# Splitting a constants load, swapping eight start-up products for six, and dropping one tiny product from a convolution loop

## What is computed

```python
x = x + attn(cond(x, cond_1024, Wx, Wh, b), A_log, D, C_re, C_im, log_dt)
x = x + ffn(cond2(x, cond_1024, W_f, b_f, W_i, b_i, W_h, b_h), router_w, ..., sw_down)
```

## Time and profile before

| what | us |
|---|---|
| median of 3 executions | 961.59 |
| lowest, highest | 960.31, 963.49 |
| profiled execution, whole | 963.19 |
| its span, first to last instruction | 961.4 |

### The profile page before, as it was taken

One profiled execution on the slowest core, in us unless ns is written; L12 is line 12 of the kernel. 1 busy time (PEld: TensorE's weight loads), 2 busy tenths in 40 slices (PEclk: granted clock), 3 DMA queues, 4 the chain that ended last, 5 costly groups with the idle time before them and its releaser, 6 DMA issues.

```text
span 961.4 us, 62897 instructions
## 1 busy us (share of the span) xinstructions
PE 914.8 (95%) x27872; PEld 760.5 (79%) x27873; DVE 405.3 (42%) x781; ACT 506.7 (53%) x1735; POOL 300.6 (31%) x324
## 2 busy tenths in 40 slices
PE   7999999999999999999999999999899999999993
PEld 5887888888888888995444446788799999999993
DVE  1000000000000004552999799775555646556450
ACT  2444444444444446543876776235456656566551
POOL 3111111111111112540004473760055464554545
PEclk7799999999999999999999999999999999999997
DMA  2222223221111111111001120532466576665634
GB/s 90 83 94 93 97 90 116 88 75 40 36 33 33 41 39 37 66 66 47 0 1 45 44 71 11 208 125 78 154 141 136 132 163 128 150 136 131 134 39 54
DMA packets 69161, 80.34 MB, mean 84 GB/s; under 512 B 24225, under 2 KB 53558, under 8 KB 69122
## 3 DMA queue, kind: packets, MB, share of 16 engines
q1 hardware_dynamic: 54242, 62.18, 20.4%
q0 software_dynamic: 14592, 17.10, 10.8%
q10 hardware_dynamic: 288, 0.56, 0.2%
HBM read 44.16 MB, written 33.83 MB: 81 GB/s over the span
## 4 chain that ended last, share of the span: by engine, by line
PE 88%; DVE 4%; ACT 3%; issue 2%; POOL 1%; DMA 0%; POOLq 0%; SPq 0%; ACTq 0%; DVEq 0%
PE ps L517 22%; PE ps L817 17%; PE ps L831 9%; PE ps L509 9%; PE ps L683 8%; PE ps L733 6%; PE ps L489 4%; PE ps L760 3%; PE ps L583 2%; PE ps L596 2%; PE ps L605 2%; PE ps L742 2%; PE ps L494 2%; ACT tok L885 1%; PE ps L569 1%
## 5 line engine op out<-in xcount | busy, mean ns | idle before, releaser
L517 PE MATMUL ps<-tok,wh 128*32 128x8 f32 x16384 | 262.2, 181 | 12.4 <-ACT tok L885 5.7
L517 PEld LDWEIGHTS ps<-tok,wh 128*32 128x32 f32 x16384 | 216.5, 112 | 65.0 <-ACT tok L885 22.8
L885 ACT ACTIVATE tok<-ps 128x8 f32<-128x8 f32 x1024 | 156.0, 178 | 191.8 <-PE ps L517 188.2
L466 POOL DMA_INDIRECT out<-arena,dest x80 | 127.8, 1598 | 98.7 <-ACT arena L1036 79.5
L418 POOL TENSOR_TENSOR big<-tok,zero 128x128 f32 x64 | 29.0, 452 | 306.0 <-ACT tok L885 306.0
L817 PE MATMUL ps<-xgT_hi,ew_hi 128*128 128x320 f32 (+1 forms) x384 | 118.8, 309 | 4.7 <-DVE mid L1387 1.8
L817 PE MATMUL ps<-xgT_hi,ew_lo 128*128 128x320 f32 (+1 forms) x384 | 118.9, 310 | 0.0
L817 PE MATMUL ps<-xgT_lo,ew_hi 128*128 128x320 f32 (+1 forms) x384 | 118.2, 308 | 0.0
L1149 DVE TENSOR_TENSOR arena<-arena,pack 128x256 f32 x32 | 13.6, 425 | 231.3 <-ACT arena L890 231.3
L1387 DVE TENSOR_TENSOR mid<-mid,ps 128x320 f32<-128x320 f32 (+1 forms) x96 | 46.7, 486 | 107.0 <-ACT mid L1054 105.0
L683 PE MATMUL ps<-mid,gw 128*128 128x512 f32 x192 | 85.5, 603 | 2.4 <-ACT mid L964 1.6
(11 more groups left out here) (206 smaller groups left out, 1614.7 us busy)
## 6 DMA issues: line engine op xcount, KB each, us to landing
slots_in<-mid SPq DMA_DIRECT2D x16, 645.0 KB, 3.8
mid<-slots_in SPq DMA_DIRECT2D x16, 645.0 KB, 4.2
arena<-in_ex_down SPq DMA_DIRECT2D x16, 384.0 KB, 3.2
arena<-in_ex_gate SPq DMA_DIRECT2D x16, 352.0 KB, 4.1
arena<-in_ex_up SPq DMA_DIRECT2D x16, 352.0 KB, 5.8
xst<-in_x_steps SPq DMA_DIRECT2D x66, 64.0 KB, 1.8
xtok<-in_x_tok SPq DMA_DIRECT2D x16, 256.0 KB, 2.8
mid<-k_pad SPq DMA_DIRECT2D x32, 128.0 KB, 3.1
```

What stands on the lines that cost most here:

```text
L466: pool.indirect_dma_start(out=out[:, :], out_offset=bass.IndirectOffsetOnAxis(ap=dest[:, z, t:t + 1], axis=0), in_=yo[:, z, t], in_offset= ...
L517: last = nc.tensor.matmul(sums_at(bank, t, o)[Q * j:Q * j + Q], wh[:, k, columns(j, o)], hring[:, (n - 1) % (2 * G), k], start=False, stop ...
L885: nc.scalar.activation(hring[:, n, o], sums_at(n // G, n % G, o), ACT.Tanh).then_inc(s_h[o], 1)
```

## The change

- pack is loaded in two parts. ACT loads the first 213 columns where it loaded all; SP loads the other 365 behind the second input steps, on a semaphore of its own (s_pack). ACT, POOL and DVE wait for it before they first use a column of the second part.
- WARM is 6 in place of 8, and the 28 small products of zeros behind the recurrence are 30.
- In the convolution, the tiny product ahead of `carried` goes with its two waits; of these, the one for the scan of the group (s_xc at m + 2) moves ahead of `block_states`, where the wait was for m + 1.

```diff
-WARM = 8
+WARM = 6
...
+        EARLIER = sum(sizes[0:4])
...
+        s_pack = sem("s_pack")
...
             sp.dma_start(xst[:, 1], x_steps[1]).then_inc(s_xs[1], 16)
+            sp.dma_start(pack[:, EARLIER:], pack_d[:, EARLIER:]).then_inc(s_pack, 16)
...
             pool.wait_ge(s_const, LOADED)
+            pool.wait_ge(s_pack, 16)
             pool.wait_ge(s_rows, 1)
...
-            for _ in range(28):
+            for _ in range(30):
                 keep_up(8)
...
                     own_block(z)
                     pe.wait_ge(s_pe, m + 2)
-                    pe.wait_ge(s_xc, m + 1)
+                    pe.wait_ge(s_xc, m + 2)
                     pe.wait_ge(s_uea, 2 * m + SLOTS - 1)
                     stand()
                     block_states(1 - z)
-                    pe.wait_ge(s_xc, m + 2)
-                    pe.wait_ge(s_uea, 2 * m + SLOTS - 2)
-                    stand()
                     carried(z)
...
-            act.dma_start(pack[:], pack_d).then_inc(s_const, 16)
+            act.dma_start(pack[:, 0:EARLIER], pack_d[:, 0:EARLIER]).then_inc(s_const, 16)
...
+            act.wait_ge(s_pack, 16)
             powers(0)
...
+            dve.wait_ge(s_pack, 16)
             with dve.Fori(0, IT) as i:
                 kernel_states(i)
```

## The result

| | median us | lowest, highest | executions |
|---|---|---|---|
| before | 962.89 | 960.31, 998.2 | 20 |
| changed | 958.85 | 956.41, 967.94 | 20 |

The ratio of changed to before is 0.9966, with a 95% interval of 0.9951 to 0.9981; times near 1000 us belong to a slow state that any kernel falls into at times, and the ratio leaves them out. So the change saves 0.34%, 3.3 us (1.8 to 4.7). Timed again (experiment 11) it was 0.9967 (0.9946 to 0.9989). The forecast was 1.8 to 1.9 us.

What follows compares the result with a forecast made beforehand. PE was taken to bound the kernel, busy 95% of the span. Start 0.50 plus convolution 1.44 (1.7 - 0.26) made 1.94 us off the median 961.59: 959.65, stated as 959.8; range 958.0 to 961.8 us.

Steps and rivals of the forecast that it cites:

- The tiny product, 1.7 us: Convolution: one tiny product fewer in each of 16 groups, 0.11 us each, saves 1.7 us (bounds 0 and 1.76).
- Rival D: Convolution: the tiny product hides a switch, so its removal gives nothing and 0.26 us stays: 961.35 us; chance 0.1.
- The wait moved ahead, 0.26 us once: Convolution: block_states waits for the previous group's scan; only group 0 pays, 0.26 us once.
- The slack of 0.9 us: Convolution: behind group 0 each scan ends about 0.9 us before PE needs it, so the moved wait costs nothing.
- Rival C: Convolution: the moved wait binds in every group, 4.2 us lost, 963.5 us; chance 0.1 together with B's slow side.
- The pack in two parts, 0.50 us: Start: 187 KB less to move before wx lands, so the first input product starts 0.50 us sooner (0 to 0.90).
- Six zeros, 0 us, 0.5 in the range: Start: zeros end 0.90 us sooner, no gain; a missed clock rise could cost up to 0.5 us, taken as 0.
- rival A: Start: clock rise missed or wx no sooner, so the start gives 0: 960.15 us, or 960.5; chance 0.2.
- The program's pieces: First 26 us: five idle pieces, PE waiting for instructions, 3.9 us apart, follow PE, each some 0.5 us sooner.
- Rival B: Clock dip behind the convolution missed: 958.0 us, chance 0.15; or rise at 35.5 us shifts, 1 us either way.

Runs made afterwards that it cites:

- experiment 11: The changed kernel, unaltered, timed again against the kernel before: ratio 0.9967 (0.9946 to 0.9989).
- Experiment 5: The changed kernel with the tiny product put back ahead of carried, without a wait; against the kernel before: ratio 0.9995 (0.9974 to 1.0015).
- 9: The changed kernel with a tiny float32 product on a 64x64 tile ahead of carried, no wait; against the kernel before: ratio 1.0083 (1.0051 to 1.0114).
- 10: The changed kernel with a tiny bf16 product on a 64x64 tile ahead of carried, no wait; against the kernel before: ratio 0.9999 (0.9969 to 1.0029).
- experiment 2: The kernel before with the start's edits alone (pack in two parts, six zeros, thirty small ones): ratio 0.9998 (0.9983 to 1.0013).
- 3: The kernel before with the pack in two parts alone, eight zeros kept: ratio 0.9999 (0.9978 to 1.0020).
- 6: The kernel before with the start's edits, two 8-column products ahead of the six zeros and 28 small ones behind the recurrence: too few executions for a ratio.
- 7: The kernel before with the start's edits, the six zeros being longer float32 ones of 171 columns: ratio 1.0021 (0.9987 to 1.0055), from three executions.
- experiment 4: The kernel before with six zeros and thirty small ones alone, the pack in one: ratio 1.0005 (0.9980 to 1.0030).
- 1: The kernel before with the convolution's edit alone (tiny product out, wait moved ahead): ratio 0.9994 (0.9972 to 1.0016).
- 8: The changed kernel with eight zeros and 28 small ones; against the kernel before: ratio 0.9975 (0.9958 to 0.9993).
- 12: The kernel before with the convolution's edit alone, timed a second time: ratio 0.9979 (0.9962 to 0.9996).

## Why the prediction was right, and where it was not

The total and its sign were right, at the edge: the saving is 3.3 us, the forecast 1.9, and the chance for more than 0.3% was put at 0.22 only. That the predicted time, 959.8 us, lies 1 us from the measured 958.85 is luck in part: the median before, 961.59 from three executions, became 962.89 with twenty, and from that the same sum gives 961.0. Point by point:

*The tiny product, 1.7 us.* This is the term that was mis-sized. It took the tiny product's own piece of the chain, 0.11 us, as the whole of its cost, with 1.76 as the upper bound. The profiles showed 0.26 us a group, 16 x 0.26 = 4.2 us. Experiment 5 shows that this belongs to the product, waits or none, and 9 and 10 that 0.16 to 0.22 of it goes when its tile is that of its neighbours. Without it the first products of carried start among the last of block_states. Rival D, that the removal gives nothing for a switch between kinds, had this the wrong way round: the switch was what the tiny product cost.

*The wait moved ahead, 0.26 us once.* Right in kind and place; it measured 0.46, and 0.44 to 0.46 in all eight profiles with the moved wait. The slack of 0.9 us held in the other 15 groups: of 16 scans only one had PE wait for it. Rival C fell. A cost that was not in the sum is the piece of the program behind group 0, which PE now reaches with less behind it: about 0.3 us in the profile of the changed kernel. (The group with that piece took 0.3 to 0.8 us more than the later ones in the six profiles with the old convolution, 0.4 to 1.6 in the eight with the moved wait.) Term by term, 4.2 - 0.46 - 0.3 = 3.4, and the stage measured 3.27. A second one is the clock's fall at some 384 us, 1.4 us where it happens; the prediction looked for such a fall only behind the convolution.

*The pack in two parts, 0.50 us.* The first input product came 0.30 us sooner in the changed kernel; with the pack split it was at 4.75 to 5.39 us in ten profiles (5.13 on the mean), with the pack in one at 5.34, 5.35, 5.50 and once at 6.45. The direction is shown; the size is about 0.3 us, with as much of scatter. The gain at the end is not resolved (experiments 2 and 3).

*Six zeros, 0 us, 0.5 in the range.* The input products and the first step took 0.4 to 0.7 us more wherever the clock did not rise early: 2.64 us from the first input product to the first tanh, against 1.91 to 2.21. That was so in six of eight profiles with six bf16 zeros and in none of five with eight such zeros or the six long ones. The price at this place was put at 0 where it was up to 0.7 in six of eight profiles, and rival A has that much right. But it did not reach even the 16th step, which was 21.2 to 22.6 us behind the first input product without the rise and 21.3 to 22.4 with it. The prediction's reason, that the program's arrival sets the pace up to 26 us, agrees with this. The Trainium skill (TensorE: Matmul & The Clock Gate, The HAM clock gate) says that sustained activity releases the clock and that the moment differs from run to run; the traces agree, for in two executions six zeros were enough (rise at 4.1 and 4.0 us).

The profiles alone mislead here, for eight zeros do not always bring the early rise. Every execution has its mean granted clock on record. In the fourteen profiled ones it is 0.969 to 0.981 with the early rise, and 0.990 to 0.993 without, where the low level at the start is not counted. Taking values below 0.985 as an early rise, it was there in 75 of 138 executions with eight zeros and in 17 of 71 with six (of the executions that the ratios use; 6 and 7, with other zeros, and 9, with no clear split, are left out). Of the kernel before, on the three chips of the experiments, executions without it had medians 1.6, 1.7 and 2.5 us above those with it. An estimate from these numbers is that six zeros cost 0.3 x 1.6 to 2.5, some 0.5 to 0.8 us, on the mean; experiment 4's 1.0005 agrees but does not resolve it. Why an early rise should go with a sooner end is not shown: in the ten profiles whose later rise is at 32 to 36 us, the recurrence ended at 364.5 to 367.8 us with it and at 364.2 to 365.6 without.

*The program's pieces.* They were there again, five of them, their ends 3.7 us apart and not 3.9. The Trainium skill (Runtime: NRT & Kernel Launch, Instruction fetch mechanics) calls this mostly hidden; the first pass through the loop disagrees, with 3.8 us of idle pieces in the changed kernel and 6.6 before.

*Rival B, the clock's changes fall elsewhere.* It was given too little. The clock's later rise, at 32 to 36 or 47 to 52 us, moves the end of the recurrence by some 3 us; the fall behind the convolution, at 433 to 442 us, was there in 6 of 14 profiles, and another at 680 to 690 us, inside the later stages, in 6 (1, 3, 4, 6, 8, 12). These are of the size of the scatter between executions of one kernel; that they make most of it was not tested. Nor are they all apart from the change: it makes an early rise rarer, and may bring the fall inside the convolution. The 2.1 us by which the recurrence ended sooner in the profile are for the most part such scatter: experiment 2, with the same start, ended it at 365.6 us, and experiment 11, with the same kernel, at 369.2.

## What to carry to other kernels

A tiny matmul that only carries a wait had better not exist: look in the chain at the products behind it, not at its own row, for it can keep them from starting among those ahead of it. Giving it its neighbours' tile made the groups 0.15 to 0.22 us shorter in the profiles, but no timing showed a gain from it, and with the float32 one the kernel was slower. A wait can often be moved to one that is there anyway, when what it waits for has slack in all iterations but the first. And where the moment at which the clock rises can move an execution by 3 us, and the first steps differ by 1.4 us between two profiles of one kernel, one profile on each side says nothing on a 3 us change: compare stages, over several profiles, and time many executions.

## What the runs showed that I had not expected

- A product of zeros of 8 columns on a tile of 128x32, between two blocks on tiles of 64x64, cost 0.26 us, one on the 64x64 tile 0.05 us in bf16 and 0.11 us in float32.
- The clock stayed at 1.2 GHz until 47 to 52 us in 4 of 14 profiles, in a loop in which PE is busy 98% of the time (7.83 of 8 us), and rose at 32 to 36 us in the others.
- By its mean over the execution, the granted clock rose early in 75 of 138 executions with eight zeros and in 17 of 71 with six, and executions of the kernel before without the early rise were 1.6 to 2.5 us slower.
- The first five packets of the program took 4.8 us in one execution and 6.8 us in another, and the first 16 steps 21.2 to 22.6 us.
- The first input product, which waits for 0.3 MB, came at 6.45 us in one execution (12), 1.1 us later than in two others of the same start.
